# A four-layer graph kernel: the row sums, the lag of the products and the order of the transposes in its first product

## The reference

```python
# layer 0: U and Vt are both adj
Vxw = adj @ (x @ weight)
out = adj @ (scale[:, None] * Vxw) + bias      # scale = sum(d_list * filt * d_list)
# layer 1: A' = alpha * adj, its diagonal raised by 1 - alpha
out = relu(((1 / A'.sum(axis=1))[:, None] * A' @ x) @ W.T + b)
# layer 2: d = 1 / sqrt(sum(A, axis=-1)); twice, the second time with 4 nearest neighbours added to A
z = leaky_relu((d[:, None] * (A @ (d[:, None] * x))) @ W1 + b1)
# layer 3
out = relu(concat([x, adj @ x]) @ W.T + b)
```

## Time and profile before

| | us |
|---|---|
| median of 3 runs | 1589.72 |
| lowest run | 1587.08 |
| the profiled execution | 1597.85 |
| span of its instructions on core 0 | 1596.3 |

### The profile page before, as it was taken

How to read it: one execution, slowest core, us unless ns; L and a number is a source line. 1 busy time by engine, 2 the same in 40 slices (tenths; PEclk the granted TensorE clock), 3 DMA queues, 4 the chain that set the end, 5 groups by cost and what they waited for, 6 DMA issues and landing times.

```text
span 1596.3 us, 20924 instructions
## 1 busy us (share of the span) xinstructions
PE 1446.2 (91%) x7300; PEld 748.6 (47%) x7300; DVE 836.0 (52%) x1278; ACT 465.3 (29%) x979; POOL 208.9 (13%) x267
## 2 busy tenths in 40 slices
PE   6888888887999999999999888999999499878997
PEld 4555555554444444444444433444444144433554
DVE  6667667664222133323222379999998046543122
ACT  4656565653000000000000056666665000000010
POOL 1111111110000000000000000000000447763000
PEclk9999999999999999999999999999999799989999
DMA  9999998888899888888777500013333889889773
GB/s 312 332 334 340 340 323 314 311 323 332 340 343 345 335 314 312 316 324 331 304 283 283 184 7 1 14 54 120 123 124 115 283 321 371 310 321 361 284 284 130
DMA packets 127677, 418.98 MB, mean 262 GB/s; under 512 B 10657, under 2 KB 44033, under 8 KB 104577
## 3 DMA queue, kind: packets, MB, share of 16 engines
q1 hardware_dynamic: 78272, 331.37, 55.9%
q0 software_dynamic: 19088, 71.83, 11.8%
q10 hardware_dynamic: 30256, 15.00, 3.2%
HBM read 353.14 MB, written 65.01 MB: 262 GB/s over the span
## 4 chain that ended last, share of the span: by engine, by line
PE 56%; DVE 16%; DMA 10%; issue 7%; POOL 5%; ACT 5%; DVEq 0%; ACTq 0%; POOLq 0%; SPq 0%
PE acc L1010 12%; PE acc L1011 12%; PE acc L1012 12%; POOL gath_all L434 5%; DVE hT L865 5%; DVE wz_sb L866 5%; DMA at_scratch<-region 4%; PE pt L1054 3%; DMA gath_all<-y_scratch,wz_sb 2%; DVE region L818 2%; PE pt L1116 2%; PE pt L1119 2%; PE pt L1118 2%; PE pt L1117 2%; PE pt L1012 2%
## 5 line engine op out<-in xcount | busy, mean ns | idle before, releaser
L1010 PE MATMUL acc<-region,yop 128*128 128x512 f16 x850 | 326.8, 385 | 63.7 <-DVE region L818 39.1
L1011 PE MATMUL acc<-region,yop 128*128 128x512 f16 x850 | 326.2, 384 | 0.0
L1012 PE MATMUL acc<-region,yop 128*128 128x512 f16 x850 | 325.8, 383 | 0.0
L592 ACT ACTIVATE region<-pt 128x512 f32<-128x512 f32 x256 | 149.8, 597 | 114.8 <-PE pt L1119 79.6
L818 DVE SCALAR_TENSOR_TENSOR region<-pt,region 128x512 f16<-128x512 f32 x200 | 128.9, 685 | 94.2 <-ACT region L499 93.5
L1054 PE MATMUL pt<-ident,region 128*128 128x128 f32 x1024 | 153.7, 278 | 8.3 <-DMA region<-in_adj 8.3
L1010 PEld LDWEIGHTS acc<-region,yop 128*128 128x128 f16 x850 | 83.6, 98 | 156.1 <-DVE region L818 51.2
L1054 PEld LDWEIGHTS pt<-ident,region 128*128 128x128 f32 x1024 | 129.7, 144 | 55.2 <-issue 9.5
L865 DVE MAX8 hT<-region 128x8 f32<-128x4096 f32 x32 | 141.5, 4421 | 11.4 <-ACT region L592 10.6
L499 ACT ACTIVATE region<-pt 128x512 f16<-128x512 f32 x200 | 112.6, 593 | 106.9 <-PE pt L1054 64.1
L1012 PEld LDWEIGHTS acc<-region,yop 128*128 128x128 f16 x850 | 83.9, 99 | 102.9 <-issue 4.4
(11 more groups left out here) (221 smaller groups left out, 1904.7 us busy)
## 6 DMA issues: line engine op xcount, KB each, us to landing
region<-at_scratch SPq DMA_DIRECT2D x180, 1280.0 KB, 7.3
region<-in_adj SPq DMA_DIRECT2D x64, 1024.0 KB, 9.0
at_scratch<-region POOLq DMA_DIRECT2D x40, 768.0 KB, 7.1
region<-at_scratch SPq DMA_DIRECT2D x100, 256.0 KB, 3.7
at_scratch<-region POOLq DMA_DIRECT2D x40, 512.0 KB, 7.5
x_scratch<-xout ACTq DMA_DIRECT2D x24, 256.0 KB, 6.2
yop<-in_x SPq DMA_DIRECT2D x4, 512.0 KB, 10.8
xin<-in_x POOLq DMA_DIRECT2D x8, 256.0 KB, 3.5
```

The costliest lines, as they stand in the source:

```text
L592: nc.scalar.activation(near[i % 2][:, j * CHUNK:(j + 1) * CHUNK], pt[n % NEAR_BANKS][:, :], ACT.Copy).then_inc(near_copied, 1)
L1010: nc.tensor.matmul(into, y[:, 0, kt, :], high, start=(kt == 0), stop=False)
L1011: nc.tensor.matmul(into, y[:, 0, kt, :], low, start=False, stop=False)
L1012: return nc.tensor.matmul(into, y[:, 1, kt, :], high, start=False, stop=(kt == KT - 1))
```

## The change

Four edits, all in pass 0 but for the place of the projection. (1) Row sums go by single row tiles: of a unit's four, DVE takes 0 and 2 at its tiles 0 and 2, ACT 1 and 3 at its tiles 1 and 3; `load_natural` waits for both engines. (2) `LAG` is 4, and the last four products of a chunk are done between the first transposes of the next; after the last chunk they follow by themselves. (3) The four transposes of a tile stand around the three matmuls of the tile four before, not ahead of them. (4) ACT copies `acc` behind tile 7, PE projects at tile 11, DVE scales at tile 14 and splits at tile 15.

```diff
-LAG = 3
+LAG = 4
+ROW_PIECES = 2
...
@@ load_natural
-                        half = c * (NAT_UNITS // 2) + (u - 4) // 2 + 1
-                        sp.wait_ge(rows_summed_dve if u % 2 == 0 else rows_summed_act, half)
+                        sp.wait_ge(rows_summed_dve, before * ROW_PIECES)
+                        sp.nop(nofuse=True)
+                        sp.wait_ge(rows_summed_act, before * ROW_PIECES)
...
@@ split_high
-                    if kt % 8 == 6:
-                        u = kt // TPC
-                        act.wait_ge(nat_loaded[u % 4], 16 * (c * 2 + u // 4 + 1))
...
-                        for t in range(TPC):
...
-                        last.then_inc(rows_summed_act, 1)
-                    if kt == 8 and not (isinstance(c, int) and c == 0):
+                    if kt % 2 == 1:
+                        u, t = divmod(kt, TPC)
+                        n = c * NAT_UNITS * ROW_PIECES + u * ROW_PIECES + t // 2
+                        if t == 1:
+                            act.wait_ge(nat_loaded[u % 4], 16 * (c * 2 + u // 4 + 1))
...
+                        if not (first(c) and u == 0):
+                            act.wait_ge(rows_summed_act, n - 1)
+                        discard = (xin, xout)[t // 2][:, :, :].rearrange("p t f -> p (t f)").bitcast(BF16)
+                        nc.scalar.activation(discard[:, 0:CHUNK], nat[u % 4][:, t, :], ACT.Copy,
+                                             accum_out=rs_part[par][:, u, t:t + 1]).then_inc(rows_summed_act, 1)
+                    if kt == 7 and not first(c):
                         act_epilogue(act, 0, c - 1, 1 - par)
...
@@ split_low
-                    if kt % 8 == 2:
-                        u = kt // TPC
-                        dve.wait_ge(nat_loaded[u % 4], 16 * (c * 2 + u // 4 + 1))
-                        nc.vector.tensor_reduce(rs_part[par][:, u, :], nat[u % 4], AXX, ALU.add
-                                                ).then_inc(rows_summed_dve, 1)
-                    if kt == 16 and not (isinstance(c, int) and c == 0):
-                        counted(0, c - 1, lambda: epilogue(0, c - 1, 1 - par))
+                    if kt % 2 == 0:
+                        u, t = divmod(kt, TPC)
+                        if t == 0:
+                            dve.wait_ge(nat_loaded[u % 4], 16 * (c * 2 + u // 4 + 1))
+                        nc.vector.tensor_reduce(rs_part[par][:, u, t:t + 1], nat[u % 4][:, t, :],
+                                                AXX, ALU.add).then_inc(rows_summed_dve, 1)
+                    if kt == 14 and not first(c):
+                        scale_projected(c - 1)
+                    if kt == 15 and not first(c):
+                        counted(0, c - 1, lambda: split_projected(c - 1))
...
-        PROJECT_AT = {0: 8, 1: 4, 2: 10, 3: 3}
+        PROJECT_AT = {0: 11, 1: 4, 2: 10, 3: 3}
...
@@ PE: products_of now takes c, par, kt and between
+                pe.wait_ge(low_done, c * KT + kt + 1)
...
+                nc.tensor.matmul(acc[par][:, :], yh, hi, start=(kt == 0), stop=False)
+                between(1)
+                nc.tensor.matmul(acc[par][:, :], yh, lo, start=False, stop=False)
+                between(2)
+                last = nc.tensor.matmul(acc[par][:, :], yl, hi, start=False, stop=(kt == KT - 1))
...
@@ transposing_chunk
                     if not (first(c) and kt < 4):
                         pe.wait_ge(low_done, c * KT + kt - 3)
...
+                    turn(0)
+                    if kt >= LAG:
+                        products_of(c, par, kt - LAG, turn)
+                    elif not first(c):
+                        products_of(c - 1, 1 - par, KT + kt - LAG, turn)
+                    else:
+                        turn(1)
+                        turn(2)
+                    turn(3)
...
-                for kt in range(KT - LAG, KT):
-                    products_of(kt)
...
             each_chunk(pe, transposing_chunk)
+            for kt in range(KT - LAG, KT):
+                products_of(NCH - 1, 1, kt, lambda t: None)
```

More of the change, by code:

```diff
@@ L303, in _ @@
             sp.wait_ge(tr_done, NCH * KT)
-            sp.wait_ge(rows_summed_dve, NCH * NAT_UNITS // 2)
-            sp.wait_ge(rows_summed_act, NCH * NAT_UNITS // 2)
+            sp.wait_ge(rows_summed_dve, NCH * NAT_UNITS * ROW_PIECES)
+            sp.wait_ge(rows_summed_act, NCH * NAT_UNITS * ROW_PIECES)
             sp.wait_ge(acc_full, NCH)
@@ L499, in split_high @@
                     nc.scalar.activation(dst, pt[kt % 4][:, :], ACT.Copy, scale=A_SCALE).then_inc(high_done, 1)
-                    if kt % 8 == 6:
-                        u = kt // TPC
-                        act.wait_ge(nat_loaded[u % 4], 16 * (c * 2 + u // 4 + 1))
-                        if u == 1 and not (isinstance(c, int) and c < 2):
-                            act.wait_ge(rows_closed, c - 1)
-                        if not (isinstance(c, int) and c == 0 and u == 1):
-                            act.wait_ge(rows_summed_act, c * (NAT_UNITS // 2) + u // 2)
-                        for t in range(TPC):
[L508 to L511, removed]
-                        last.then_inc(rows_summed_act, 1)
-                    if kt == 8 and not (isinstance(c, int) and c == 0):
+                    if kt % 2 == 1:
[3 more added lines that the diff above has]
+                            act.wait_ge(nat_loaded[u % 4], 16 * (c * 2 + u // 4 + 1))
+                        if kt == 1 and not (isinstance(c, int) and c < 2):
+                            act.wait_ge(rows_closed, c - 1)
+                        if not (first(c) and u == 0):
[4 more added lines that the diff above has]
+                    if kt == 7 and not first(c):
                         act_epilogue(act, 0, c - 1, 1 - par)
@@ L715, in epilogue @@
                 dve.wait_ge(nat_full, n)
[L716 to L720, removed]
                 if p == 1:
@@ L806, in _, with scale_projected, split_projected @@
             y0_part(0)
+            def scale_projected(c):
+                dve.wait_ge(nat_full, nth(ALL, 0, c))
+                nc.vector.tensor_tensor(t_nat[:, :, :], pnat[:, :, :], per_row(scale, c), ALU.mult).then_inc(nat_read, 1)
+            def split_projected(c):
+                dve.wait_ge(nat_read, nth(ALL, 0, c))
+                split(0, t_nat[:, :, :], c)
             def split_low(c, par, m):
@@ L825, in split_low @@
                         setup_copies()
-                    if kt % 8 == 2:
-                        u = kt // TPC
-                        dve.wait_ge(nat_loaded[u % 4], 16 * (c * 2 + u // 4 + 1))
-                        nc.vector.tensor_reduce(rs_part[par][:, u, :], nat[u % 4], AXX, ALU.add
-                                                ).then_inc(rows_summed_dve, 1)
-                    if kt == 16 and not (isinstance(c, int) and c == 0):
-                        counted(0, c - 1, lambda: epilogue(0, c - 1, 1 - par))
-                dve.wait_ge(rows_summed_dve, (c + 1) * (NAT_UNITS // 2))
-                dve.wait_ge(rows_summed_act, (c + 1) * (NAT_UNITS // 2))
+                    if kt % 2 == 0:
[8 more added lines that the diff above has]
+                        counted(0, c - 1, lambda: split_projected(c - 1))
+                dve.wait_ge(rows_summed_dve, (c + 1) * NAT_UNITS * ROW_PIECES)
+                dve.wait_ge(rows_summed_act, (c + 1) * NAT_UNITS * ROW_PIECES)
                 nc.vector.tensor_reduce(rs[:, bass.ds(c * TPC, TPC)], rs_part[par][:, :, :].rearrange("p u t -> p t u"),
@@ L837, in _ @@
             each_chunk(dve, split_low)
-            counted(0, NCH - 1, lambda: epilogue(0, NCH - 1, 1))
+            scale_projected(NCH - 1)
+            counted(0, NCH - 1, lambda: split_projected(NCH - 1))
             close(0)
@@ L1027, in setup_transposes, with stored @@
                 nc.tensor.transpose(setup_rows, hT[0:rows_j, 0:P], ident[0:rows_j, 0:rows_j]).then_inc(setup_pe, 1)
-            def transposing_chunk(c, par, m):
[L1030 to L1045, removed]
+            def stored(c, par, kt):
+                if kt < KEPT:
+                    return [kept[:, bass.ds(c, 1), kt, h, :].rearrange("p c n -> p (c n)") for h in range(2)]
+                s = (par * UPC + (kt - KEPT) // UNIT) % 2
+                return [stage[s][:, (kt - KEPT) % UNIT, h, :] for h in range(2)]
@@ new lines, in products_of @@
+            def products_of(c, par, kt, between):
+                hi, lo = stored(c, par, kt)
+                pe.wait_ge(low_done, c * KT + kt + 1)
+                if first(c) and kt % XT_PART == 0:
+                    pe.wait_ge(y0_ready, kt // XT_PART + 1)
+                if kt == 0 and not (isinstance(c, int) and c < 2):
+                    pe.wait_ge(hT_ready, c - 1)
+                yh, yl = (yop[OPERAND[0]][:, h, kt, :] for h in range(2))
+                nc.tensor.matmul(acc[par][:, :], yh, hi, start=(kt == 0), stop=False)
[3 more added lines that the diff above has]
```

(13 more changed lines are left out.)

2 lines of the change are left out of this document (removed).

## The result

The changed kernel takes 1551.02 us (median of 4 runs, 1547.55 to 1554.99) against 1592.13 for the kernel before (median of 4 runs, one of which took 2805.07; without it the median is 1589.72). The ratio on record is 0.9723, 95% interval 0.9686 to 0.9761; the quotient of the two medians, 0.9742, lies within it. The profiled execution took 1550.28, its span is 1548.7. The forecast was 1550.

The account below looks back on a forecast made before the run. PE isn't full in the first product: some 10 us a chunk lost waiting on DVE, ACT and stores. Savings of 35, 3 and 2.5, together 40, take 1597.85 to 1558 profiled, 1550 us on the runs' scale; range 1528 to 1592.

Parts of the forecast that it names:

- Chunks 1 to 6 save 35 us: First product: each of these six chunks goes from 45.8 to 40.0 us, paced by DMA.
- rival B: First product: loads catch up in the kept tiles, a chunk nears 36.1 to 37 us, 1530 in all; chance 0.15.
- It can't be full all the time: DMA in a chunk: 7 kept tiles store nothing, so 25 stored tiles at 1.28 us set the pace, 40.0 a chunk.
- Chunk 0 saves 3, the last 2.5: First product's outer chunks: the first saves its end and part of the later bursts, the last its projection wait, in us.
- Lag over chunk ends, 16 us: Seven chunk ends of the first product: a lag of four removes 2.3 us at each.
- (a): Chunk's end: four row sums in a burst, then PE finishes three products with nothing to transpose; excess 2.3 us.
- (b): Tiles 6 to 9: four row sums delay the copy of acc, PE stands 1.87 us; excess 3.4, elsewhere about 2.5.
- (d): Rest of the 10 us lost a chunk, about 2, at the later bursts and DVE's epilogue of tile 16.
- The chain of 3.1 us in 3.3 fits: Last transpose to product through high and low half, with one row sum each on ACT and DVE, fits three PE blocks.
- C: Rival: the round trip binds, PE waits some 0.3 us a block, 45 us a chunk, 1584 in all; chance 0.08.
- SP's later release costs nothing: SP waits for all row-sum pieces of a unit, some 1.5 us later; put at nothing, bound 0 to 1 us a chunk.
- D: Rival: interleaved weight loads come uncovered, 0.42 us more a tile, 49.2 a chunk, 1617 in all; chance 0.05.

Follow-up runs that it names:

- small stores: Changed kernel with each store from chunk 1 on cut to 512 columns of 3072 or 2048, so values differ from the reference; 1547.97 us on a slower chip.
- e_straight: Changed kernel with the eight chunks of the first product written out on all five engines, no loop; ratio 0.9642 to the kernel before.
- b_cross: Kernel before with only the lag of four that crosses chunk ends added; 1573.82 us, ratio 0.9851.
- ahead_again: Changed kernel with the four transposes ahead of the three products again, timed beside the changed kernel on one chip; 1545.34 us, ratio 0.9678.
- u_drain: Changed kernel with the last four products done at each chunk's end, nothing beside them; 1547.74 us, ratio 0.9692.
- u_rows: Changed kernel with the row sums by units again (DVE at tile 2, ACT at tile 6 of each eight); 1562.27 us, ratio 0.9773.

## Why the prediction was right

The time, 1550 for 1551.02, was right, and that it is right to 1 us is luck: three errors cancel. I had put 40 us of saving on the profiled execution, 1597.85, and the first product saved 52.2. Of the 12 us more, 4.6 were lost in the later products, and about 8 went with my step from the profiled execution to the median: I took 8 us off since the profile before was slow by that much, but the profiled execution after, 1550.28, is within 1 us of its median, where the forecast for it was 1558. The count of 0.40 for four fifths of 0.48 should be 0.38, which changes no verdict.

- *What bounds the kernel*: right. PE's floor of 35.7 us a chunk is measured as 35.5 by the small stores. DMA is what is late next: leaving out most of the stores ends the stage 13.9 us earlier.
- *Chunks 1 to 6 save 35 us*: 39.1 measured, by 39.3 a chunk where 40.0 was forecast. The mechanism of that term failed. I had 1.28 us a tile in the 25 stored tiles, from the landing of the stores, and waits for stores of 60 us. They fell to 20.8, the stored tiles went at about 1.2 us, and the queues stayed full in the kept tiles as well, with the loads' landing 1.1 us later. That is what rival B said, which I gave 0.15: the rate was 385 to 405 GB/s outside the stalls, and 14.94 MB at 395 is 37.8 us, the pace of `e_straight`. The step that failed is "It can't be full all the time". The kept tiles of a chunk show it, in the kernel before and in the changed one:

```profile
288.00:295.00 7.00, 6.00 (x40) 4.18 (x39) 6.33 (x8) 4.99 (x12) 0.00 (x0) 1.00 0.74 250
```

```profile
206.00:214.00 8.00, 8.00 (x52) 5.79 (x50) 7.81 (x15) 6.77 (x17) 1.07 (x2) 1.00 1.03 416
```

- Against that stood a term that I didn't have: two stalls of 5.25 and 4.51 us at the loop's end. Without them the six chunks would sum to 226 of 236 us by subtraction, 228 by `e_straight`.
- *Chunk 0 saves 3, the last 2.5*: 7.7 and some 5 (from 49.8 to 42.1, and to 44.6 in the second execution; from 42.4 between first high half and last copy to 37.3). Mis-sized, since I took only the terms I could name there and not the row sums' bursts.
- *Lag over chunk ends, 16 us*: 18.5 alone, right; 6.8 when it is taken back from the changed kernel.
- *Row sums by tile*: named as the removal of bursts (a), (b) and (d), and at 35.9 alone the largest part. Taken back it is 16.8, so it overlaps the lag. The parts alone, 35.9 and 18.5, are already more than the whole, 52.2. I read it so that the burst at tile 30 and the drained end are one wait, and whichever edit removes it is given the gain; that is argued. A second reason is on record: the sums by tile bring the stalls at the loop's end with them, and taking them back takes those away too.
- *The chain of 3.1 us in 3.3 fits* (against C): PE waits 3.3 us for the low halves of `stage` in all. *SP's later release costs nothing*: waits for adj went up by 3.7 us in all, inside its bound of 8. It wasn't tried by itself, and the 17.8 of the second execution are 9.5 up, but 13.4 of them are in chunk 0, where `b_cross`, which has the old release, waits 12.1.
- *Interleaved transposes cost nothing* (against D): 1.08 a tile, loads covered; 1.4 and 1.7 us of the stage, not told from nothing.
- The stage gained 52 us and the kernel 41 to 48. From the last copy to the end of the span the profiled executions have 1220 us before, 1224 and 1224 in the two of the changed kernel, and 1211 to 1224 in the others but those of the chip with 1631.67, which have 1236 to 1251; nothing is edited there but the projection's place. The first 1000 us of it are the same (PE busy 941.72 before, 942.23 and 941.54 in the changed kernel and `ahead_again`, and 943.23 in `e_straight` on the slower chip). The difference lies in the 100 us behind them, in PE's wait for the operand of the last product, here in the changed kernel and in `ahead_again`:

```profile
PE acc L1235 <- DVE yop L663: 18.4, 2, 13.4
```

```profile
PE acc L1232 <- DVE yop L663: 9.3, 3, 5.3
```

  It is 13.1 us in the kernel before, 17.1 in the second execution of the changed kernel, and 7.2 in `u_drain`, which has the shortest rest, 1211. So in their profiled executions `ahead_again` and `u_drain` are faster than the changed kernel mostly by a wait 1000 us behind the edit. What moves that wait stays open.

## What to carry to other kernels

Work that an in-order engine does in a burst between the links of a pipeline costs more than its own time: cut it into pieces that fit the slack of one step, and it can be free at the same total (here DVE spent no less on its sums, and the stage got 36 us shorter). When several stalls share one chain, measure each edit alone and taken back; they don't add. Compare a stage by marks at both its ends: the first chunk alone moved the last mark by up to 4.7 us here. And look for the next bound as a rate over a whole period, since a queue with slack on one side (here the loads) can move its work to where the engines were idle.

## What the runs showed of the hardware that I had not expected

A loop's end can cost an engine 3.4 to 5.7 us. With the sums by tile ACT stands still there, and packets of the instruction queue are in flight just then (165:172 of the changed kernel):

```profile
q14 instruction: 3, 0.02, 1.1%
```

From the loop's second round on, this queue tells the kernels apart. In 180:320 the changed kernel still has

```profile
q14 instruction: 6, 0.05, 0.1%
```

and the others with sums by tile and ACT's loop have 6 to 8 packets; the kernel before, `u_rows` and `b_cross`, with the sums by units, have none on it.

With the sums by units ACT's loop has no such stall in any chunk (`u_rows`, `b_cross`, and the kernel before), and with ACT's chunks written out the two stalls of 5 us are gone. The Trainium skill (Runtime: NRT & Kernel Launch, section "Instruction fetch mechanics") says that prefetch of instructions is sequential and that a taken branch to a target outside the window held on chip forces a fetch by DMA. These rows agree with it: the loops that stall are those that fetch in every round. That ACT's loop outgrew the window by the semaphore waits of the single sums is argued, not shown: how long a loop may be was not tried.

A DVE sum of 512 elements takes 676 ns in its rows, but the next instruction starts 0.59 us after it, so the estimate of 0.6 from a quarter of 2276 held:

```profile
163.22 0.68 DVE L834 TENSOR_REDUCE rs_part<-region 128x1 f32<-128x512 f32 x1
...
163.81 1.42 DVE L822 SCALAR_TENSOR_TENSOR region<-pt,region 128x512 f16<-128x512 f32 x2
```
